# Local attention of six layers: the weighing's operands changed places, the exps divided by their sum before they are turned, and a new TensorE order

## The reference, cut to what matters

```python
for i in range(DEPTH):                      # 6
    x = attn_layer(shift_tokens(x), Wqkv[i], q_scale[i], k_scale[i], Wo[i]) + x
    x = ffn_layer(shift_tokens(x), ...) + x

# in attn_layer and local_attention: 16 heads of 64, windows of 32 queries,
# each of which looks at its own 32 keys and at the 32 before
sim = einsum('bhwie,bhwje->bhwij', bq, bk2) * QK_SCALE      # scores
attn = softmax(where(mask, -inf, sim), -1)                  # over 64 keys
out = einsum('bhwij,bhwje->bhwie', attn, bv2)               # "the weighing"
return out.transpose(...).reshape(b, n, INNER) @ Wo
```

## Time and profile before

| | us |
|---|---|
| median of three runs | 4915.28 (4913.58 to 4918.22) |
| the profiled execution's own time | 4913.37 |
| its span | 4911.6 |
| PE busy | 4324.2 (88%) |
| PEld busy | 3033.4 (62%) |
| DVE busy | 3368.4 (69%) |
| ACT busy | 2512.7 (51%) |
| POOL busy | 1965.2 (40%) |
| granted TensorE clock, mean | 0.952 |

### The profile page before, as it was taken

The page is one execution under the profiler, slowest core; times in us unless marked ns, Lnnn a source line. Parts: engine busy times, 40 slices in busy tenths (PEclk is TensorE's granted clock), DMA queues, the critical chain, the costliest instruction groups (busy, mean ns, idle before and its releaser), DMA issues. The chain is left out here.

```text
span 4911.6 us, 176146 instructions
## 1 busy us (share of the span) xinstructions
PE 4324.2 (88%) x69458; PEld 3033.4 (62%) x69459; DVE 3368.4 (69%) x7024; ACT 2512.7 (51%) x5545; POOL 1965.2 (40%) x2045
## 2 busy tenths in 40 slices
PE   8999964967799988999889998999989998899986
PEld 5777742655466655666556665666656666566663
DVE  3555534167688857888578885888758887688866
ACT  4555543312466635666356663666536665366642
POOL 0000000010566625666166661666526665266641
PEclk9999976979899999999999999999989999999998
DMA  1000000300433303333033330333213332133311
GB/s 38 4 5 4 2 1 20 93 7 0 101 67 67 67 27 72 67 67 67 19 73 68 68 65 24 76 68 68 58 37 70 67 67 51 46 70 67 67 42 35
DMA packets 453921, 243.53 MB, mean 50 GB/s; under 512 B 41158, under 2 KB 447892, under 8 KB 452116
## 3 DMA queue, kind: packets, MB, share of 16 engines
q1 hardware_dynamic: 453140, 232.66, 21.2%
HBM read 35.40 MB, written 4.19 MB: 8 GB/s over the span
## 5 line engine op out<-in xcount | busy, mean ns | idle before, releaser
L1949 POOL TENSOR_TENSOR n_pre<-n_tt 128x512 f32<-128x512 f32 x768 | 971.2, 1275 | 893.5 <-DVE n_tt L2446 893.5
L2446 DVE TENSOR_TENSOR n_tt<-n_pp,n_rot 128x1024 f32<-128x1024 f32 x768 | 921.8, 1220 | 378.9 <-ACT n_sq L2295 378.9
L1963 POOL TENSOR_TENSOR n_pre<-n_pre,n_rn 128x512 f32<-128x512 f32 x768 | 776.6, 1042 | 276.3 <-ACT n_rn L2303 276.3
L2044 PE MATMUL n_pp<-n_wqkv,n_xT 128*128 128x512 f32 x1536 | 787.6, 614 | 10.9 <-ACT n_xT L2290 10.1
L2295 ACT ACTIVATE n_sq<-n_pp 128x512 f32<-128x512 f32 x768 | 459.1, 598 | 588.0 <-PE n_pp L2044 577.6
L2453 DVE TENSOR_REDUCE n_ss<-n_sq 128x8 f32<-128x512 f32 x768 | 518.4, 675 | 0.0
L2315 ACT COPY n_qkT<-n_pp 128x512 f32<-128x512 f32 x768 | 436.5, 594 | 136.7 <-PE n_pp L2060 136.6
L2060 PE MATMUL n_pp<-ident,n_pre 128*128 128x128 f32 x3072 | 436.1, 275 | 19.3 <-POOL n_pre L1963 14.3
L2074 PE MATMUL n_pp<-n_wo,n_OT 128*128 128x128 f32 x3072 | 402.1, 285 | 57.9 <-ACT n_OT L2321 57.9
L2060 PEld LDWEIGHTS n_pp<-ident,n_pre 128*128 128x128 f32 x3072 | 363.5, 143 | 130.4 <-issue 126.7
L2074 PEld LDWEIGHTS n_pp<-n_wo,n_OT 128*128 128x128 f32 x3072 | 365.1, 195 | 102.4 <-ACT n_OT L2321 101.8
(11 more groups left out here) (260 smaller groups left out, 7438.4 us busy)
## 6 DMA issues: line engine op xcount, KB each, us to landing
n_V<-n_Vn SPq DMA_DIRECT2D x768, 128.0 KB, 2.6
n_Vx<-n_Vn SPq DMA_DIRECT2D x384, 128.0 KB, 2.5
n_Vx<-n_Vn SPq DMA_DIRECT2D x576, 64.0 KB, 2.2
n_wqkv<-in_L_ffn_Wqkv SPq DMA_DIRECT2D x6, 1536.0 KB, 6.8
e_w<-in_L_ffn_w SPq DMA_DIRECT2D x32, 256.0 KB, 3.0
m_Y<-e_ye SPq DMA_DIRECT2D x64, 64.0 KB, 2.0
n_wo<-in_L_ffn_Wo SPq DMA_DIRECT2D x6, 512.0 KB, 7.2
a_xs<-in_L_attn_x SPq DMA_DIRECT2D x16, 128.0 KB, 2.1
```

The source lines that it names most:

```text
L1949: nc.gpsimd.tensor_tensor(d, s[0], s[1][:, :, ::-1, :], ALU.add).then_inc(s_add, 1)
L1963: nc.gpsimd.tensor_tensor(d, d, bcast(rn[:, j, t, 8 * half:8 * half + 8], 2, D), ALU.mult).then_inc(s_kn, 1)
L2044: nc.tensor.matmul(pp[:, c % 2, :], xT[:, j * P:(j + 1) * P], wqkv[:, t * I + 512 * half:t * I + 512 * half + 512], start=True, stop=True) ...
L2446: nc.vector.tensor_tensor(tt[:, c % 4, :, :].rearrange("p s (h d) -> p s h d", d=D), bcast(pp[:, c % 2, :].rearrange("p (h d) -> p h d", d ...
```

## The change

The values become the loaded operand of the weighing (64 keys x 64 channels), and the turned exps the moving one (64 keys x 32 queries). The result comes out turned, channels on the partitions, as `output` needs it. So `turn_output`, its two banks, the tile `On` and `norm_output` go; `copy_output` copies `pW` straight into `OT`. The exps are divided by their sum in `norm_weights`, on VectorE, in place in `E`, ahead of `turn_weights`. A multiplication of the weighing now takes 64 rows x 64 columns of the array, of which there are four. `turn_weights` of a half moves behind the first projection of the next half, and `weigh` behind the next half's `scores`; ScalarE's copies follow. The wait for the weighing two sequences back moves from `copy_v` on ScalarE to SyncE, ahead of the DMAs that place the values.

```diff
             def turn_weights(N, j):
+                after(pe, s_OT, 4 * N + 2 * j)
                 for e in range(2):
-                    after(pe, s_On, 4 * N + 2 * j)
-                    after(pe, s_E, 4 * N + 2 * j + e + 1)
+                    after(pe, s_En, 4 * N + 2 * j + e + 1)
...
             def weigh(u, j):
                 for c in range(4):
-                    for e in range(2):
-                        for w in range(NW):
-                            m = (NW * j + w) // 2
-                            v = V if w % 2 else Vx
+                    for w in range(NW):
+                        m = (NW * j + w) // 2
+                        v = V if w % 2 else Vx
+                        for e in range(2):
                             o = c * P + e * D
                             for f in range(2):
                                 r = D * f
-                                last = nc.tensor.matmul(pW[W * w:W * w + W, f, o:o + D],
-                                                        ET[r:r + D, e, c, W * w:W * w + W],
-                                                        v[r:r + D, u, m, o:o + D], start=True, stop=True)
+                                last = nc.tensor.matmul(pW[D * e:D * e + D, f, c * P + W * w:c * P + W * w + W],
+                                                        v[r:r + D, u, m, o:o + D],
+                                                        ET[r:r + D, e, c, W * w:W * w + W], start=True, stop=True)
...
                     masks(N, j)
-                    if j == 1:
-                        weigh(u, 0)
-                    elif prev:
-                        weigh(1 - u, 1)
                     if nxt:
                         project_qk(N + 1, 4 * j)
+                    for n, v, k in behind:
+                        turn_weights(n, k)
+                    if nxt:
                         project_qk(N + 1, 4 * j + 1)
...
                     scores(j)
-                    if j == 1:
-                        turn_output(N, 0, bank("o", 0, 0))
-                        turn_output(N, 1, bank("o", 1, 0))
...
+                    for n, v, k in behind:
+                        weights_ready(pairs[0], n, v, k)
+                        held(pe, s_held)
+                        weigh(v, k)
                     if prev:
                         output(N - 1, j, bank("y", j, -1))
...
-            def norm_output(N, j):
+            def norm_weights(N, j):
                 after(dve, s_ri, 2 * N + j + 1)
-                after(dve, s_OTp, 4 * N + 2 * j)
-                after(dve, s_PV, 4 * N + 2 * j + 2)
-                r = ri[:, j, :, :].rearrange("p e (c f) -> p f c e", f=2)
-                for f in range(2):
-                    nc.vector.tensor_tensor(On[:, f, :].rearrange("p (c e d) -> p c e d", c=4, e=2),
-                                            pW[:, f, :].rearrange("p (c e d) -> p c e d", c=4, e=2),
-                                            bcast(r[:, f, :, :], 3, D), ALU.mult).then_inc(s_On, 1)
+                for e in range(2):
+                    x = E[:, e, :].rearrange("p (i s) -> p i s", s=2 * W)
+                    nc.vector.tensor_tensor(x, x, bcast(ri[:, j, e, :], 2, 2 * W), ALU.mult).then_inc(s_En, 1)
...
                     sum_exps(N, j)
+                    norm_weights(N, j)
                     if nxt:
-                        for c in (4 * j + 2, 4 * j + 3):
-                            rotate(N + 1, c)
-                            sum_squares(N + 1, c)
+                        rotate(N + 1, 4 * j + 2)
+                        rotate(N + 1, 4 * j + 3)
+                        sum_squares(N + 1, 4 * j + 2)
+                        sum_squares(N + 1, 4 * j + 3)
```

More of the change, by code:

```diff
@@ L1816, in l1_network @@
         s_ri = sem("sums_inverted")
+        s_En = sem("weights_normed")
         s_ETp = sem("weights_turned")
@@ L2028, in freed @@
                     after(pe, s_qkT, 8 * N + c + 1)
-                elif kind == "o":
-                    after(pe, s_OT, 4 * N + c + 1)
                 elif kind == "y":
@@ L2061, in turn_qk @@
                 last.then_inc(s_turn, 1)
-            def turn_output(N, k, bank):
-                j, f = k // 2, k % 2
-                after(pe, s_On, 4 * N + k + 1)
-                for c in range(4):
-                    last = nc.tensor.transpose(pp[:, bank, c * P:(c + 1) * P], On[:, f, c * P:(c + 1) * P],
-                                               ident[:, :])
-                last.then_inc(s_OTp, 1)
             def output(N, j, bank):
@@ L2201, in attention @@
                     weigh(u, 1)
-                    output(N, 0, bank("y", 0, 0))
-                    turn_output(N, 2, bank("o", 2, 0))
-                    turn_output(N, 3, bank("o", 3, 0))
                     output(N, 1, bank("y", 1, 0))
```

61 lines of the change are left out of this document (24 added, 37 removed).

## The result

The changed kernel takes 5196.81 us (median of 4 executions, 5167.84 to 5200.26), the kernel before beside it 4914.43. The ratio is 1.056, 95% interval 1.052 to 1.060: 282 us slower. The forecast was 4969 with a range of 4860 to 5050, so the direction was right and the size far off. The profiled execution spans 5193.5 us.

The account below looks back on a forecast made before the run. TensorE was taken as the bound, with stops at instruction-block borders. A half: 10.35 + 4.8 + 0.4 = 15.55 us against 15.10, +81 us; layer ends -27; sum +54, giving 4969 us, range 4860 to 5050.

Parts of the forecast that it names:

- A block entered in a burst needs 3.4 us until the next one: TensorE's instruction fetch: a 256-instruction block entered in a small-tile burst delays the next block's entry to 3.4 us later.
- The double burst: Scores and weighing now adjoin, 512 instructions in nearly every half: 4.8 us in the mean, with stops for instructions.
- Rival A: The instruction fetch keeps up: scores and weighing together 3.4 us, half 14.15 us, 4717 us in all; chance 0.10.
- 14.5 ns for a wide load and multiplication: Weighing with 64x64 tiles: load and multiplication overlap, 14.5 ns a pair, 128 pairs, 1.86 us.
- rival C: Wide tiles don't overlap load and multiplication: weighing 2.8 us, half 16.0 us, 5050 us in all; chance 0.15.
- The sign: Whole kernel: slower than before, chance 0.62; faster 0.28, same 0.10.
- D: Rival: the parts cancel, half 15.25 us, within the bound of no change; chance 0.10.
- B: Rival: fetch costs as forecast, VectorE's chain hidden, other steps a tenth shorter: half 14.95 to 15.0 us, 4870 us; chance 0.18.
- The halves' clock was taken as 1.00: TensorE's granted clock in the halves: full, as in the profile before; a lower one named as upsetting the sum, unpriced.
- the wait at the first projection: Next half's first projection waits for VectorE's `rotate` behind norm_weights: 0.5 us, or 0.2 in a half with turn_x.
- The layer ends: Last half with its tail 20.4 us, the half before 10 to 11: -4.5 us a layer, -27 us in all.
- the rule on row groups: The skill's rule: a load overlaps running multiplications only if its row group differs; said to cost near 3 us a half.

Follow-up runs that it names:

- run 3: Changed kernel with the weighing's operands and loops as before the change, in the new order; result not the reference's: 5092.47 us, 1.037.
- run 2: Changed kernel with the output of the sequence before moved between scores and weighing, ScalarE's exps ahead of copy_output: 4797.84 us, 0.977.
- run 10: run 5 with the second v projection (eight instructions, 0.9 us) moved between scores and weighing: 4845.97 us, 0.985.
- run 12: Changed kernel without the weighing's first quarter (64 of 256 instructions), result not the reference's: 4977.26 us (one execution).
- run 6: Changed kernel with output between scores and weighing, and turn_weights ahead of the first projection: 4730.1 us, 0.963.
- run 5: Changed kernel with turn_weights ahead of the half's first projection, ScalarE's copies of the weights ahead of its square: 5094.82 us, 1.039.
- run 1: Changed kernel with VectorE's norm_weights moved behind the rotate of the third projection: 5288.62 us, 1.078.
- Runs 4: run 2 with one wait more: TensorE waits for both exps of the half ahead of the weighing: 5147.8 us, 1.049.
- 13: run 6 with TensorE waiting ahead of the weighing's third quarter for VectorE's reciprocal: 5275.74 us, 1.075.
- runs 8: run 6 with the first two turnings of q and k moved ahead of the weighing: 4956.32 us, 1.008.
- 11: Changed kernel's operands and early division, TensorE's order near the old one, output behind scores, third projection between the first two turnings of q and k: 4925.0 us, 1.002.
- 14: run 6 with the second v projection too between scores and weighing, behind the output: 4690.95 us, 0.954.
- runs 9: run 6 with the weighing's operands and loops as before the change; result not the reference's: 4665.97 us, 0.949.

## Why the prediction was right and wrong

Right, with the numbers of the halves at full clock:

- *A block entered in a burst needs 3.4 us until the next one.* The double burst takes 4.8 us, as forecast. It held against less work per instruction (3), more distance (2, 10) and another count of instructions (12). The mean hides two small errors that cancel: 2 of a layer's 31 double bursts have no stop, not 5, and the bursts with one are a little shorter than forecast. Rival A is out, since its 4717 us needs the bursts apart (run 6: 4730), and with it the sentence of the Trainium skill ("Runtime: NRT & Kernel Launch", section "Instruction fetch mechanics") that a crossing is mostly hidden.
- *14.5 ns for a wide load and multiplication.* Where no stop falls into it the weighing's groups of eight loads stand 0.11 to 0.12 us apart; rival C's 2.8 us are not there.
- *The sign*: the double burst eats what TensorE won, 1.38 us a half for turn_output against 1.74 for the weighing. D and B are out.

Wrong, in the order of size (span 5193.5 against before 4911.6, +282; forecast +54; 228 us to explain). A usual half is any but a layer's first and its last two, 174 in all:

- *The halves' clock was taken as 1.00*, 141 us. This is the step that failed. The prediction's last paragraph says that a lower clock would upset the sum, "since TensorE now stands still for up to 2 us at a time", and then gives it no price, no chance and no place in the range. The runs showed 283 us at a granted clock of 0.50. The trace of the kernel before had the sign. Timeline and busy time by stretch at the end of layer 1:

```profile
1757.24 0.24 PE L2119 MATMUL n_pW<-n_Vx,n_ET 64*32 64x64 f32 x2 [2.36 <-issue]
...
1757.51 3.48 PE L2074 MATMUL n_pp<-n_wo,n_OT 128*128 128x128 f32 x16
1762.95 2.02 PE L2074 MATMUL n_pp<-n_wo,n_OT 128*128 128x128 f32 x16 [0.87 <-ACT n_OT L2321]
```

```profile
1757.88:1761.29 3.41, 3.41 (x19) 3.41 (x18) 1.47 (x3) 0.00 (x0) 0.00 (x0) 0.50 0.02 5
```

  A stop for instructions of 2.36 us, and 0.6 us behind it 3.41 us at half clock: the output takes 3.48 us, and 2.02 the next time. All six layers end so, with the fall 0.4 to 0.9 us behind the stop; it is the 0.92 of the last row. The six stops of 2.1 us in the scores, of which the prediction read one, have none behind them.
- *The usual half at full clock* was forecast 0.45 us longer than before and is 0.85 longer, 148 us instead of 81. The time from one step's start to the next one's, in usual halves at full clock:

| step | before | forecast | changed |
|---|---|---|---|
| masks and the wait behind them | 0.53 | 0.80 | 1.15 |
| six projections | 5.38 | 5.15 | 5.36 |
| scores and weighing | 3.07 | 4.8 | 4.80 |
| turnings of q and k | 2.04 | 1.79 | 1.91 |
| turn_output | 1.38 | 0 | 0 |
| whole half | 15.24 | 15.55 | 16.09 |

  The steps left out differ by 0.1 us or less. The failed terms are the wait at the first projection, where the duration of turn_x is right (0.22) but not the cover that its move took from the copy of xT (0.85 us in 90 halves, and the wait named was `rotate`), the projections at 0.43 us a pass, 0.2 too short in sum, and the second turning (0.17 instead of 0.05). Against that the forecast compared a usual half with the mean of 15.10, which has the short ends of a layer in it; the usual half before took 15.24.
- *The layer ends*, the remaining 19 us: -27 was forecast for the last half with its tail and the half ahead of it. A layer's first and next to last halves gain 13 us in sum, the 2100 us outside the 186 halves lose 5. The last half with its tail is 1.1 us longer in the mean, with 3.4 or 6.8 us of it at low clock, where 1.5 less were forecast.

Two passages of the prediction don't come out and change nothing. By its own 5.2 and 5.5 us, the rule on row groups would make the change cost 0.3 us a half, not near 3. And rival B's half of 14.95 us needs the other steps 0.2 us shorter, not a tenth of their 10.35.

What stays open: why about half of the 99 stops of 1.5 to 2 us bring a fall and the others not. Their place plays a part. Of those that begin within 2.4 us of the double burst's start 32 of 46 bring one, of the later ones 15 of 48 (tails left out); run 5 has 36 of 52 and 21 of 57, but run 1 the reverse, 9 of 50 and 19 of 53. It is open too why fewer come with the old tiles (run 3), and why the stop at one and the same border is 1.06 us long in one layer and 1.80 in another; what else the DMA queues carry was not varied. Runs 4, 5, 10 and 13 say where the fall comes and from about what length, not by what measure.

## What to carry to other kernels

Count instructions, not only microseconds: two dense bursts of small tiles side by side can be bound by the fetch of TensorE's program, and 1 to 3 us of long instructions moved in between gave 250 to 400 us here. When a step moves, list what it covered at its old place and what it needs covered at its new one: runs 8 and 11 lost to that, as the change itself did, and in run 1 the moved step met another engine. And a stop of 1.5 us or more amid small tiles can bring a second bill, at half clock behind it, so a forecast with such stops needs a term for it. Look at the granted clock behind each long stop that the kernel already has: here six of them told it.

## What the runs showed of the hardware

- TensorE's stops stand a multiple of 256 of its instructions apart (168 of 168 stretches in the changed kernel, 114 of 114 in run 12), and two adjoining bursts of 256 small instructions take 4.8 us instead of 3.1, with a stop of 1.7 us in the mean. 0.9 us of other work between them shortens it to 0.9 us (134 stops, run 10), 2.0 us leave 12 stops (run 2).
- The granted clock falls to 0.50 in stretches of 3.41 us (or 6.8) behind stops amid small-tile work: 502 us in one kernel (13), 7 in another with the same loads and multiplications (14).
- Loads and multiplications of 64x64 tiles run at 14.5 ns a pair, 64x32 at 11 ns: groups of eight loads stand 0.11 to 0.12 us apart, and the weighing takes 1.75 us with the old tiles and 2.1 with the new (runs 9 and 6).
- A division 128x512 out of and into SBUF takes 688 ns alone and 1186 in the mean where GpSimd works beside it.
